# Extra TensorE products of constants ahead of three routing steps and ahead of the first expert

## The reference

```python
x = x + 0.5 * ffn(layernorm(x))
x = x + attention(layernorm(x))      # 16 heads, causal, latent size 64
x = x + 0.5 * ffn(layernorm(x))
```

```python
shared = silu(xf @ sg) * (xf @ su) @ sd
pos = cumsum(onehot(flat_e))[...] - 1;  keep = pos < 320
buf[e, pos] = xf[tok]
out_e = (silu(buf @ wg) * (buf @ wu)) @ wd          # per expert, 128 -> 256 -> 128
routed[tok] += out_e[e, pos] * gate * keep
```

## Time and profile before

| what | us |
|---|---|
| median of 3 runs | 1122.03 |
| lowest and highest run | 1119.82, 1126.57 |
| the profiled execution's own time | 1125.98 |
| its span, first to last instruction | 1124.2 |
| TensorE busy in the span | 904.0 (80%) |
| VectorE busy in the span | 569.0 (51%) |

### The profile page before, as it was taken

The page is one execution under the profiler, slowest core; times in us unless marked ns, Lnnn a source line. Parts: engine busy times, 40 slices in busy tenths (PEclk is TensorE's granted clock), DMA queues, the critical chain, the costliest instruction groups (busy, mean ns, idle before and its releaser), DMA issues.

```text
span 1124.2 us, 16448 instructions
## 1 busy us (share of the span) xinstructions
PE 904.0 (80%) x5179; PEld 734.7 (65%) x5179; DVE 569.0 (51%) x1644; ACT 409.8 (36%) x809; POOL 330.6 (29%) x326
## 2 busy tenths in 40 slices
PE   2306599999379889999999799599999937999983
PEld 2204276777237778988886688488888725777663
DVE  8431144444356776665652676267446514444443
ACT  1100122222144555555642455346435522222223
POOL 1736515555400000000000014531000262455551
PEclk9998799999779999999999899799999978999996
DMA  9800225444252021223120021210202102444525
GB/s 344 284 23 28 62 67 151 146 154 147 93 196 58 19 48 29 48 83 106 25 53 10 1 61 48 79 42 21 56 10 48 44 25 58 136 135 149 158 92 190
DMA packets 97475, 99.09 MB, mean 88 GB/s; under 512 B 15225, under 2 KB 82699, under 8 KB 96646
## 3 DMA queue, kind: packets, MB, share of 16 engines
q1 hardware_dynamic: 88198, 85.98, 25.7%
q0 software_dynamic: 9216, 12.33, 3.5%
HBM read 58.62 MB, written 38.60 MB: 86 GB/s over the span
## 4 chain that ended last, share of the span: by engine, by line
PE 56%; DVE 15%; another core or an unknown queue 12%; issue 10%; ACT 3%; DMA 2%; POOL 1%; SPq 1%; DVEq 0%; POOLq 0%; ACTq 0%
PE PS L1593 19%; PE PS L1551 6%; PE PS L1472 5%; PE PS L1576 5%; PE PS L1473 4%; DVE mxp L1167 3%; PE PS L1485 2%; PE PS L1639 2%; PE PS L1493 2%; DVE xs L1149 1%; ACT area_o L741 1%; PE PS L1554 1%; DMA yg<-ybuf 1%; PE PS L1579 1%
## 5 line engine op out<-in xcount | busy, mean ns | idle before, releaser
L1593 PE MATMUL PS<-pT,area_v 128*128 128x256 f32 (+1 forms) x1280 | 305.2, 362 | 4.8 <-ACT area_o L779 4.8
L1167 DVE TENSOR_REDUCE mxp<-PS 128x2 f32<-128x512 f32 (+1 forms) x320 | 197.0, 630 | 139.9 <-PE PS L1551 67.0
L820 ACT ACTIVATE pT<-PS 128x512 f32<-128x512 f32 (+1 forms) x320 | 176.6, 553 | 235.8 <-PE PS L1579 113.9
L1593 PEld LDWEIGHTS PS<-pT,area_v 128*128 128x128 f32 x1280 | 213.9, 194 | 19.0 <-ACT area_o L779 5.1
L657 POOL DMA_INDIRECT ybuf<-area_o,yidx x160 | 155.4, 971 | 162.8 <-DVE area_o L1126 78.4
L643 POOL TENSOR_TENSOR area_o<-area_o,rden 128x512 f32<-128x512 f32 x31 | 39.5, 1273 | 494.0 <-DMA rden<-den 493.7
L1551 PE MATMUL PS<-Kz,Qx 128*128 128x256 f32 (+1 forms) x640 | 168.6, 356 | 18.6 <-DVE mxp L1167 11.3
L613 POOL DMA_INDIRECT xbuf<-xn,sidx x128 | 124.9, 976 | 112.5 <-issue 59.8
L1576 PE MATMUL PS<-Qx,Kz 128*128 128x256 f32 (+1 forms) x640 | 144.0, 307 | 5.4 <-ACT pT L820 2.3
L1551 PEld LDWEIGHTS PS<-Kz,Qx 128*128 128x128 f32 x640 | 113.8, 197 | 40.8 <-DVE mxp L1167 16.0
L1472 PE MATMUL PS<-area_o,area_v 128*128 128x320 f32 x256 | 97.3, 462 | 22.4 <-ACT area_o L741 17.4
(11 more groups left out here) (174 smaller groups left out, 898.5 us busy)
## 6 DMA issues: line engine op xcount, KB each, us to landing
area_v<-xbuf SPq DMA_DIRECT2D x32, 340.0 KB, 3.3
area_v<-in_L_ffn_wg_dram SPq DMA_DIRECT2D x32, 256.0 KB
area_v<-in_L_ffn_wu_dram SPq DMA_DIRECT2D x32, 256.0 KB
area_v<-in_L_ffn_wd_dram SPq DMA_DIRECT2D x64, 128.0 KB
rden<-den SPq DMA_DIRECT2D x248, 32.0 KB
yg<-ybuf SPq DMA_DIRECT2D x24, 256.0 KB, 4.6
qkbuf<-stage SPq DMA_DIRECT2D x24, 256.0 KB, 3.7
xbuf<-Kz SPq DMA_DIRECT2D x4, 1360.0 KB, 12.3
```

Of the source, the lines that this page charges most:

```text
L820: nc.scalar.activation(pT[:, N % 4, 0:w], PS[:, 2 + N % 2, 0:w], ACT.Exp).then_inc(exp_done, 1)
L1167: nc.vector.tensor_reduce(mxp[:, i, c, 2 * hp:2 * hp + 2], PS[:, k % 2, 0:2 * w].rearrange("p (h w) -> p h w", h=2), AX.X, ALU.max).then_i ...
L1593: ins = mm(PS[:, pv_bank(U, a), (p + 1) * TC - w:(p + 1) * TC], value_and_ones(j, h), pT[:, N % 4, a * w:(a + 1) * w], start=(N in UNIT_FI ...
```

## The change

A helper `keep_busy(n)` is added to TensorE's program. It issues n fp32 products of the 128x128 identity with 256 columns of constants (both parts of the loaded constants `cst`) into the first 256 columns of bank 3 and announces nothing. Nobody reads what it writes; `shared(0)` later starts that bank afresh. It is called with 8 products ahead of the first counts, 8 ahead of the second, 7 behind them, 8 ahead of the third counts, 3 behind them, and 8 ahead of `experts(0)`, where a wait for `sh_x` 4, the one with which `experts` itself begins, is put ahead of it. These are 42 products, each with two weight loads and two MATMULs.

```diff
--- before.py
+++ after.py
@@ -1639,6 +1639,11 @@
                     ins = mm(o, yT[:, c, i * P:(i + 1) * P], wo_in[:, c, :], start=False, stop=(c == 7))
                 return ins
 
+            def keep_busy(n):
+
+                for _ in range(n):
+                    mm(PS[:, 3, 0:TC], ident, cst[:, C_ID:C_ID + TC], start=True, stop=True)
+
             pe.wait_ge(s_const, 16)
             ln_half(0, 0, 0)
             pe.wait_ge(s_cnn, 1)
@@ -1649,13 +1654,17 @@
             scores(1, 0)
             pe.wait_ge(s_cst, 1)
             for f in range(2):
+                keep_busy(8)
                 counts(f)
+            keep_busy(7)
             pe.wait_ge(xnT_ready, 2)
             ln(1, 1)
             pe.wait_ge(sc_read, 1)
             scores(2, 1)
             pe.wait_ge(slot_ready, 1)
+            keep_busy(8)
             counts(2)
+            keep_busy(3)
             pe.wait_ge(s_w, N_W)
 
             pe.wait_ge(slot_ready, 3)
@@ -1672,6 +1681,8 @@
             ins.then_inc(s_wk, 1)
             pe.wait_ge(s_ax, 1)
             shared(0)
+            pe.wait_ge(sh_x, 4)
+            keep_busy(8)
             experts(0)
             for h in range(2):
                 ln_half(2, 0, h)
```

## The result

| | before | after |
|---|---|---|
| median of 20 runs each, us | 1123.75 | 1127.77 |
| lowest to highest | 1116.80 to 1127.31 | 1122.87 to 1131.27 |
| ratio, 95% interval | | 1.0035 [1.0019, 1.0052] |
| profiled execution: span, mean granted clock | 1124.2, 0.944 | 1122.8, 0.917 |
| TensorE busy in the span | 904.0 | 928.3 |

The change costs 4.0 us, 2.1 to 5.9 by the interval. It is small, but clear of noise, and in the direction of the forecast. The profiled execution of after happens to be a short one, so the spans say nothing about it; where the time went has to be read inside the trace. Nor does the mean granted clock say that the change slowed TensorE. The column reads 1.00 in the trace of before until 103 us, and in that of after only until 32 us; over the first 150 us it gives 0.93 and 0.74, behind them 0.95 in both.

The account below looks back on a forecast made before the run. It took GpSimd's scatter trains, and their start, to set the time up to the experts, not TensorE. First call +2.2 and last call +3.4 sum to 5.6 us over 1122.03: 1127.6 us, range 1119 to 1133.

Parts of the forecast that it names:

- The forecast: Whole kernel: first call +2.2 and last call +3.4 both cost, 5.6 us in sum, near 1127.6 us; chance 0.57.
- The last call on the path: Ahead of the experts: 8 products at 0.43 us each, at the full clock, add 3.4 us.
- The first call slips the train: Ahead of the first counts: counts, and GpSimd's first scatter behind them, slip by 2.2 us; lower bound 0.
- when the clock rises: First call: TensorE starts at 1.2 GHz and rises after 3.6 to 5.2 us of products, so counts slip 1.6 to 3.2.
- The reading of the durations against the clock column: Around 20 us: durations show 1.2 GHz early on; the column's 1.00 was taken for a missing record.
- from there on equal durations: Sign in the profile after: L1446 some 5.6 us later than 149.97, and equal durations behind it.
- Calls two to five: Around the second and third counts: four calls covered by waits or other engines' work, cost 0 each.
- The bound of the stretch: Routing to experts: GpSimd's scatter trains set the time; VectorE and ScalarE follow their ends by 4.63 and 4.64 us.
- "slower" rival: First call: TensorE's instructions come late, 16 MATMULs take 17.6 us; +17.5 in all, 1139.5 us; chance 0.07.
- VectorE's signals explain the transposes' pace: Argument against late instructions: VectorE's signals explain as well the eight transposes from 42.23 us, one per 1.1 us.
- Quick signals: Third scores: busy TensorE lets VectorE go at 54.8, not 72.27; -17.5 + 5.6 = -11.9 us, 1110.1; chance 0.09.
- A warm fold: Behind the third counts: 3 products raise the clock, fold saves 5.8 us; -0.2 in sum, 1121.8; chance 0.05.

Follow-up runs that it names:

- again: The changed kernel run once more with no edit, in another group of runs against the kernel before: ratio 1.0028 [1.0010, 1.0046], +3.1 us.
- The dose of 32: The changed kernel with 32 instead of 8 products ahead of the experts: ratio 1.0133 [1.0111, 1.0155] against before.
- The dose of 24: The changed kernel with 24 instead of 8 products ahead of the first counts: ratio 1.0096 [1.0076, 1.0116] against before.
- 40 products: The changed kernel with 40 instead of 8 products ahead of the third counts: ratio 1.0062 [1.0039, 1.0085] against before.
- the pause: The kernel before, with GpSimd waiting after 20 of the first train's 32 scatters until VectorE has read the third scores: ratio 0.9964 [0.9941, 0.9987].
- the kernel with the early fold: The kernel before, with TensorE's fold moved ahead of the third counts and no pause in the scatters: ratio 0.9949 [0.9929, 0.9970].
- the last call only: The changed kernel with all calls removed but the 8 products ahead of the experts: 1118.38 against 1116.42 us, ratio 1.0014 [0.9995, 1.0032].
- pause and fold together: The kernel before, fold moved ahead of the third counts, GpSimd pausing after 20 scatters until it is done: 1099.86 against 1116.22 us, ratio 0.9844.

## Why the prediction was right, point by point

**The forecast**, 1127.6 for 1127.77 measured (+5.6 for +4.0 [2.1, 5.9]), is closer on the first pair than it deserves. The median of before moved up by 1.7 us with more runs, and the cost came out 1.6 lower; that the two cancel is luck. What counts is the difference: +4.0 and, again, +3.1.

**The last call on the path: right.** Expected 3.4. From last sum to transposes it took 3.61 or 3.62 us in the five traces with eight products there, against 0.05 in before. The dose of 32 confirms the slope.

**The first call slips the train: right in kind, half as large.** I took +2.2 and got +1.15, with first counts at 24.30 and first scatter at 28.02, just outside of the 24.6 to 26.2 and 28.5 to 30 that were to show it. The mis-sized step is when the clock rises. I bounded it by 3.6 to 5.2 us of products; 5.08 us for 8 products solves to a rise 3.3 us after 19.39 (2.6 in the second trace of the changed kernel), and the score products that had been running since 13.95 may have helped (not tested). The reading of the durations against the clock column was right; with the column's clock the counts would have started at 23.04. The dose of 24 shows that the slip passes on.

**Is it passed on in the time, too?** For 7 us it is. For 1.15 us that is not resolved: the kernel with the first five calls but not the last measured 0.9994 [0.9978, 1.0011]. The sum of the two halves, +0.9 us, lies below the whole's +4.0 and +3.1, but each part is uncertain by about 2 us. Part of the slip may be lost in the 5 us by which the shared layer's tail wanders. The sign "from there on equal durations" could not be read either, as the rest of the kernel alone differs by up to 14 us between traces.

**Calls two to five: free in their sizes, but for a wrong reason in one case.** The calls ahead of the second counts and behind the second and third were covered as said. The one ahead of the third counts was covered by less than I wrote: its cover starts where the third scores end, 46 to 55 us without the calls in the routing and 63 to 76 with them. I had started it at 54.74. 40 products did not fit.

**The bound of the stretch: right that the trains set it, wrong on how.** "4.6 us behind the last scatter" is no fixed lag: VectorE resumed 3.2 us behind the last scatter ahead of the pause, 3.0 behind the first train in the kernel with the early fold (67.51 to 70.47), and 3.6 with the last call only (67.59 to 71.20). ScalarE's first Silu step behind the second train fits better: 4.41 to 4.71 us in seven traces with whole trains, but 3.21 in after and 3.92 with the 40 products. Instructions that come late, which I had as the "slower" rival, are real, though what makes them late is open. I had put them under the zero-filling transfers at 20 us, where TensorE ran at full pace, instead of under the scatters. There the first train shows them from about 41 us on. One sign of it I explained away: "VectorE's signals explain the transposes' pace" does not hold. VectorE's last `xn` of that part was done at 43.58, and five transposes still came at 45.65, 46.36, 47.76, 48.47 and 49.88, steps of 0.70 and 1.40 us.

**Quick signals: refuted** as I put it. VectorE did not go sooner in any kernel with more TensorE work. The 17.5 us that this rival named for the second train were there, but it takes GpSimd, not TensorE, to release them: the pause brought that train's end forward by 16.7 us. That pause and fold together gave 17.4 us in the time is another sum.

**A warm fold: not seen.** Three products did not raise the clock: the column reads 0.50 from 84 to 90 us, and the fold's first 16 MATMULs took 3.57 us after as before. Behind the dose of 40 products the column read 1.00 until 100 us and fell as the fold began; its first 16 took 3.29.

## What to carry to other kernels

Filler products on TensorE cost their full length wherever they stand behind the wait that ends last, and their "free" places are only as wide as the wait is stable: read the cover from several traces, and from traces with the filler in. Before warming an engine, ask whether its clock bounds the stretch; here the longest waits of the routing lay under GpSimd's indirect transfers, and no kernel with more TensorE work shortened them. Where waits have no named releaser, look at what else runs through all of them, and move that. A pause of 9.8 us in the scatters, with other engines' work moved into it, bought 17 us; a shorter pause alone (4.6 us) bought 4, the moved work alone 6.

## What the runs showed of the hardware

- While GpSimd issues indirect transfers back to back (one per 1.28 us), and for up to 5 us behind the last, other engines' instructions come at multiples of about 0.70 us, with no wait recorded between them: TensorE one MATMUL per 2.80 us (paused kernel), per 2.10 (early fold), per 0.70 (four count products after the change). ScalarE's Silu steps, which also need TensorE and VectorE, came 8.40 us apart (111.28, 119.68 and 128.08 in the kernel with the last call of 32).
- It sets in with a delay: in the paused kernel TensorE ran 42 MATMULs of the fold at full pace under the train, from 71.42 to 80.88 us, before the first slow one. A stock of instructions that runs dry, as the expectation for the early fold has it, does not fit that trace. The page of its profile lists two DMA queues that bring instructions (packets, MB, share):

```profile
q8 instruction: 34, 0.56, 0.2%
q14 instruction: 27, 0.22, 0.1%
```

A packet of the first came at 72 us, and none of either queue between 73 and 145. In that time TensorE had its slow stretch (82 to 107 us), and then ran 96 MATMULs with 96 weight loads at full pace (119.96 to 144.1), without anything new being brought. Nor was transfer bandwidth used up: the DMA share in the slow stretch was 0.05 to 0.10. What holds the instructions back stays open. The Trainium skill, Runtime: NRT & Kernel Launch, section "Instruction fetch mechanics", says that an engine's instructions are fetched over a DMA queue in blocks of 16 KiB while it executes, at a cost that is mostly hidden. The trace agrees on the blocks (34 packets with 0.56 MB); the slow stretch is not such a fetch, as none was under way.
- The granted-clock column reads 1.00 from the start of these traces until its first change, though the clock was at times the lower one: 16 equal MATMULs took 5.28 and 3.67 us under the same 1.00.
